# Attention row maxima begun two groups ahead, a first block's last maxima over three PSUM bank pairs, and column sums behind the next projection

## What is computed

```python
xn = group_norm(x, gn_weight, gn_bias)                      # 32 groups
qkv = einsum('oc,bchw->bohw', qkv_weight, xn) + qkv_bias    # 4 heads of 64 channels, 4096 pixels
attn = einsum('bhdk,bhdq->bhkq', q, k) / sqrt(64)
attn = softmax(attn, axis=-1)
out = einsum('bhkq,bhdq->bhdk', attn, v)
out = einsum('oc,bchw->bohw', proj_weight, out) + proj_bias
x1 = x + out        # then BN, relu, 3x3 conv with sign weights, twice, + x1
```

## Time and profile before

| | |
|---|---|
| median of 3 runs | 3069.19 us (3068.3 to 3076.0) |
| profiled execution | 3075.72 us, span 3073.9 us |
| PE busy | 2829.9 us (92%) |
| DVE busy | 2145.2 us (70%) |
| POOL busy | 2025.5 us (66%) |
| ACT busy | 1390.7 us (45%) |
| mean granted TensorE clock | 0.972 |

### The profile page before, as it was taken

The page is one execution under the profiler, slowest core; times in us unless marked ns, Lnnn a source line. Parts: engine busy times, 40 slices in busy tenths (PEclk is TensorE's granted clock), DMA queues, the critical chain, the costliest instruction groups (busy, mean ns, idle before and its releaser), DMA issues. The chain is left out here.

```text
span 3073.9 us, 43595 instructions
## 1 busy us (share of the span) xinstructions
PE 2829.9 (92%) x17060; PEld 1013.5 (33%) x17060; DVE 2145.2 (70%) x2528; ACT 1390.7 (45%) x1461; POOL 2025.5 (66%) x1208
## 2 busy tenths in 40 slices
PE   5799999997999999987999999987999999979898
PEld 3233333323333333333333333342333333334343
DVE  5677777736777777546777777456777776488785
ACT  3354444452545444532544454543454445344342
POOL 2588778783888888843888888855878888520022
PEclk9899999998999999998999999998999999989999
DMA  5000000001000000041000000010000000232032
GB/s 203 33 1 1 1 1 1 1 1 60 1 1 1 1 1 1 1 132 54 1 1 1 1 1 1 1 42 1 1 1 1 1 1 1 71 116 88 0 109 82
DMA packets 26819, 78.27 MB, mean 25 GB/s; under 512 B 1920, under 2 KB 2176, under 8 KB 25600
## 3 DMA queue, kind: packets, MB, share of 16 engines
q1 hardware_dynamic: 25792, 74.19, 6.9%
q10 hardware_dynamic: 832, 1.45, 0.1%
HBM read 58.86 MB, written 16.78 MB: 25 GB/s over the span
## 5 line engine op out<-in xcount | busy, mean ns | idle before, releaser
L492 POOL TENSOR_TENSOR acc_pool<-acc_pool,prob 128x512 f32<-128x512 f32 (+1 forms) x992 | 1779.6, 1794 | 376.9 <-ACT prob L544 269.9
L544 ACT ACTIVATE prob<-ps,exp_scale 128x1024 f32<-128x1024 f32 x1024 | 1091.9, 1111 | 1191.0 <-PE ps L688 1188.5
L788 DVE TENSOR_REDUCE m_part<-ps 128x2 f32<-128x1024 f32 x896 | 1095.2, 1222 | 477.6 <-PE ps L648 453.6
L672 PE MATMUL ps<-prob,vals 128*64 128x512 f32 x4096 | 999.8, 609 | 0.0
L648 PE MATMUL ps<-k_hi,q_hi 64*128 64x512 f16 x1792 | 347.5, 384 | 79.8 <-DVE m_part L788 79.8
L672 PEld LDWEIGHTS ps<-prob,vals 128*64 128x64 f32 x4096 | 250.3, 137 | 498.5 <-issue 367.4
L844 DVE TENSOR_TENSOR ps<-ps,prob 128x512 f32<-128x512 f32 x480 | 331.5, 691 | 91.2 <-ACT prob L544 91.2
L683 PE MATMUL ps<-q_hi,k_hi 64*128 64x512 f16 x2048 | 391.8, 379 | 0.0
L683 PE MATMUL ps<-q_hi,k_lo 64*128 64x512 f16 x2048 | 391.0, 378 | 0.0
L683 PE MATMUL ps<-q_lo,k_hi 64*128 64x512 f16 x2048 | 390.8, 378 | 0.0
L688 PE MATMUL ps<-m_rows,shift 64*128 64x512 f16 x2048 | 390.4, 378 | 0.4
(11 more groups left out here) (115 smaller groups left out, 1587.8 us busy)
## 6 DMA issues: line engine op xcount, KB each, us to landing
xt<-in_x SPq DMA_DIRECT2D x40, 512.0 KB, 4.0
xf<-in_x SPq DMA_DIRECT2D x4, 2048.0 KB, 17.0
x_scratch<-y_tile SPq DMA_DIRECT2D x16, 512.0 KB, 5.0
wf<-in_w_t SPq DMA_DIRECT2D x4, 1152.0 KB, 9.9
rows<-x_scratch SPq DMA_DIRECT2D x8, 576.0 KB, 5.1
rows<-x_scratch SPq DMA_DIRECT2D x8, 544.0 KB, 4.6
xn<-in_x SPq DMA_DIRECT2D x8, 512.0 KB, 5.7
xt<-x_scratch SPq DMA_DIRECT2D x4, 1024.0 KB, 5.1
```

What stands on the lines that cost most here:

```text
L492: nc.gpsimd.tensor_tensor(acc[:, part], acc[:, part], tile[:, part], ALU.add).then_inc(pool_add, 1)
L544: nc.scalar.activation(prob[:, n % PBUF], g.ps_s[:, kt % 2].rearrange("p h n -> p (h n)"), ACT.Exp, scale=g.exp_scale[:]).then_inc(exp_don ...
L672: last = mm(g.ps_o[own[h], :], vals[:, kt, own[h]], prob[:, n % PBUF, h * TB:(h + 1) * TB], start=(kt == 0), stop=(kt == KT - 1))
L788: v.tensor_reduce(m_part[:, :, u], g.ps_max, AX.X, ALU.max).then_inc(mx_used, 1)
```

## The change

- `units_of` gives two units to every group, for the pair's blocks in one sequence that runs LEAD = 2 groups ahead; the third units of groups 6 and 11 are gone, and a block's last unit is reduced in group 13, where `negate_max` now stands. m_part has two slots.
- Projection step kb has the units of key block kb-1, from kb = 1 on; steps 4 to 7 have a fifth ("early") unit, of the next block, between the two matmuls of q. Four units are left behind the last step; they go to ps_max, the two pairs of the score banks, and ps_max again.
- Vectors m_neg go through ps_misc instead of ps_max, so `max_rows` waits for `half_copied`. `copy_half` moves from key tile 1 of the next block to key tile 29 of its own; the 16 halves of DVE are key tiles 11 to 26.
- ACT, not DVE, copies v. ACT normalises a pair's first two inputs ahead of the softmax of block 6 of the pair before. Four small ACT copies per pair are gone.
- A pair's last column sums stand behind the first projection step of the next pair, and at an image's end behind the first two output projections; DVE divides there ahead of the next pair's maxima, and behind the first two residuals.

```diff
-MID_AT = (6, 11)
+LEAD = 2
 ROWS_AT = GROUPS_A - 1
+NEGATE_AT = GROUPS_A - 1 - LEAD
...
+def units_of(qb, group):
+    at = [(qb + 1) * UNITS + 2 * (group + LEAD) + i for i in range(2)]
+    return [(a // UNITS, a % UNITS) for a in at if a < NB * UNITS]
+
+def units_beside(kb):
+    own = [(0, t * NB + kb - 1) for t in range(QT)]
+    return own, [(1, kb - (NB - 2 * LEAD))] if kb >= NB - 2 * LEAD else []
...
-DVE_HALVES = [kt for kt in range(11, KT - 2) if kt not in (15, 20, 25)]
+DVE_HALVES = list(range(11, 27))
+HALF_AT = 29
...
+                act.wait_ge(g.proj_ready, 4 + (pn + 1) * 3)
+                nc.scalar.activation(vals[:, (n2 * 2 + s) * QT:(n2 * 2 + s + 1) * QT, :],
+                                     ps_v[s].rearrange("p (t d) -> p t d", t=QT), ACT.Copy).then_inc(v_copied, 1)
...
                     if kt == 1 and not first:
-                        copy_half(it - 1)
                         copy_output(it - 1)
+                    if kt == HALF_AT:
+                        copy_half(it)
...
                     for qb in range(NB):
+                        if qb == NB - 2 and it0 + NB < 2 * B * NB:
+                            normalize_first((b * 2 + hp + 1) // 2, 1 - hp)
                         softmax(it0 + qb, qb == 0, qb == NB - 1)
...
+                these, early = units_beside(kb) if kb else ([], [])
+                if kb > 1:
+                    pe.wait_ge(hi_ready, 2 * (it0 + kb - 1))
                 for j in range(2):
                     for c in range(CB):
                         ins = mm(g.ps_s[:, s, j], wst[:, c, j, :], xn[:, s, c, :], start=(c == 0), stop=(c == CB - 1))
...
-                        if maxima and c:
-                            first_maxima(it0, n2 - 1, s, [j])
+                        if j == 0 and c == 0:
+                            maxima_of(it0, early)
+                        if kb and c:
+                            if j == 0:
+                                pe.wait_ge(hi_ready, 2 * (it0 + kb))
+                            maxima_of(it0, these[j:j + 1])
...
+            def last_first_maxima(it0):
+                units = units_beside(NB)[0]
+                pe.wait_ge(hi_ready, 2 * (it0 + NB))
+                pe.wait_ge(mx_used, 1 + it0 * UNITS + PLACE[units[0]])
+                maximum(it0, units[0], g.ps_max)
+                maximum(it0, units[1], g.ps_s[:, 0])
+                maximum(it0, units[2], g.ps_s[:, 1])
+                pe.wait_ge(mx_used, 1 + it0 * UNITS + PLACE[units[1]])
+                maximum(it0, units[3], g.ps_max)
...
                     scores(it, qb, kt, first)
-                    next_maxima(it + 1, qb + 1, mid)
                     scores(it, qb, kt + 1, first)
-                    next_maxima(it + 1, qb + 1, early)
+                    maxima_of(it0, units[0:1])
                     if group == ROWS_AT and not last:
+                        pe.wait_ge(half_copied, it + 1)
                         max_rows(it + 1)
...
-                    next_maxima(it + 1, qb + 1, late)
+                    maxima_of(it0, units[1:2])
...
-                    for s in range(2):
-                        project(b, hp, 0, s, False)
+                    project(b, hp, 0, 0)
+                    if hp:
+                        column_sums(it0 - 1)
+                    project(b, hp, 0, 1)
...
-                    for s in range(2):
-                        first_maxima(it0, NB // 2 - 1, s, range(QT))
+                    last_first_maxima(it0)
...
-                    column_sums(it0 + (NB - 1))
...
                     for s in range(2):
                         output_projection(b, n2, s, 1)
+                    if n2 == 0:
+                        column_sums(b * 2 * NB + 2 * NB - 1)
...
+                    if hp:
+                        for part in range(NP):
+                            divide(it0 - 1, part)
+                    for kb in range(1, NB):
+                        project_step(it0, kb)
...
                 for n2 in range(NB // 2):
+                    if n2 == 1:
+                        for part in range(NP):
+                            divide((b + 1) * 2 * NB - 1, part)
                     for s in range(2):
                         residual(b, n2, s)
```

More of the change, by code:

```diff
@@ L595, in _, with project @@
             mm = nc.tensor.matmul
[L597 removed]
+            def project(b, hp, n2, s):
                 it0 = (b * 2 + hp) * NB
@@ L621, in project @@
                                   start=(c == 0), stop=(c == CB - 1))
-                    if maxima and t == 1:
-                        first_maxima(it0, n2 - 1, s, [2])
+                    if t == 1:
+                        maxima_of(it0, these[2:3])
                 last.then_inc(g.proj_ready, 1)
[L625 to L650, removed]
+                maxima_of(it0, these[3:4])
@@ new lines, in maximum, with maxima_of @@
+            def maximum(it0, unit, into):
+                block, u = unit
+                t, kb = u // NB, u % NB
+                for h in range(2):
+                    last = mm(into[:, h], q_hi[own[h], block * TB + t * P:block * TB + (t + 1) * P],
+                              k_hi[own[h], kb * TB:(kb + 1) * TB], start=True, stop=True)
+                last.then_inc(mx_ready, 1)
+            def maxima_of(it0, units):
+                for unit in units:
+                    pe.wait_ge(mx_used, 1 + it0 * UNITS + PLACE[unit])
+                    maximum(it0, unit, g.ps_max)
@@ L848, in query_block @@
                 first, last = qb == 0, qb == NB - 1
+                it0 = it - qb
                 for group in range(GROUPS_A):
-                    mid, early, late = ([], [], []) if last else units_of(group)
-                    next_maxima(it + 1, mid)
-                    next_maxima(it + 1, early)
+                    units = units_of(qb, group)
+                    maxima_of(it0, units[0:1])
                     if group == ROWS_AT and not last:
@@ L858, in query_block @@
                         divide(it - 1, DIVIDE_AT[group, 0])
-                    next_maxima(it + 1, late)
-                    if group == ROWS_AT - 1 and not last:
+                    maxima_of(it0, units[1:2])
+                    if group == NEGATE_AT and not last:
                         negate_max(it + 1)
@@ L864, in query_block @@
                         divide(it - 1, DIVIDE_AT[group, 1])
-                if last:
-                    for part in range(NP):
-                        divide(it, part)
             def residual(b, n2, s):
```

108 lines of the change are left out of this document (48 added, 60 removed).

## The result

The changed kernel takes 2934.47 us (median of 4 runs, 2933.86 to 2936.92), beside 3068.74 us for the kernel before in the same comparison (3060.0 to 3076.0): a ratio of 0.9564, 95% interval 0.9546 to 0.9581. It is faster by 134 us. The forecast was 2932, in a range of 2912 to 2968. The profiled execution of after took 2934.27 us with a span of 2932.5, so the two profiled spans differ by 3073.9 - 2932.5 = 141.4 us, against 139.8 in the sum of the prediction. The mean granted clock rose from 0.972 to 0.988.

A forecast was written before the change was run, and what follows sets the result against it. TensorE (PE), busy 92% of the span, bounds the kernel. Terms -101.3 + 2.7 + 19.2 - 38.8 - 7.6 - 14.0 = -139.8 us take the profiled 3075.7 to 2935.9, lowered to a forecast of 2932 us, range 2912 to 2968.

The forecast's parts named there:

- Steady blocks: Blocks 1 to 6 of each pair: even spacing saves 3.24 us per block, 24 x 3.24 = 77.8 us.
- two times 0.22: Group 15 of a block: PE's cost of the two units that come back there, leaving 3.5 of 3.93 us saved.
- DVE staying late: Second rival: lag behind the division isn't cleared, groups 7 to 13 each pay 0.26 us; time 2987, chance 0.07.
- POOL trailing: Third rival: POOL's fifteen whole tiles in a row slow down and exponentials stall; slower, about 3110 us, chance 0.02.
- The clock dips: Slow-clock spells after group 6's waits in six of 28 blocks end with their cause: 6 x 1.63 = 9.8 us.
- First blocks: First block of each pair, without a division: 2.55 us saved each, four times 10.2 us; cold start left unchanged.
- Early units: Projection steps 4 to 7: an extra unit costs 1.2 us per step, 16 times, +19.2 us.
- The tail: Behind the last projection step: four units instead of eight, 8.0 us for 17.7, saving 9.7, four times 38.8.
- Pair to pair: Last values to next pair's step 2: 16.2 us for 20.0, saving 3.8, twice 7.6 us.
- Done about then or sooner, taken 0: Column sums' wait for POOL's total at a pair end, asked at 5.2 us: 0 to 0.4 us, taken 0.
- Image ends: Output projections begin at the values' end, last residual at 33.0 us behind them; 7.0 us saved, twice 14.0.
- The first rival: Early units and step 1's added wait eat the tail's saving; price 38.5 us, time 2974, chance 0.05.

The follow-up runs named there:

- the two together: The changed kernel with a lead of one group, the negation's factor folded into the mask, and DVE's division one slot earlier: 2920.71 us, ratio 0.9514.

## Why the prediction was right, and where its terms were off

The time was 2.5 us from the forecast, and the cause was the one given: the even spacing carried 91 us, shown by taking it away, the ends 20 and the three bank pairs of the tail some 10. That the shorter tail carries the rest, less what the early units cost, is read from the timeline; only the early units were varied, in the kernels with a lead of one. Point by point:

- **Steady blocks.** 71.12 - 3.24 = 67.88 was worked out, 67.75 measured. The wait that is left is where it was put, at group 6 behind the division: 4.37 from group 5, for 4.13 + 0.26. The 0.1 between the sums is in "two times 0.22": the two groups around the rows grew from 8.48 to 8.80 us, by 0.32 and not by 0.44. The rivals of DVE staying late and of POOL trailing left no trace: there is no wait in groups 7 to 13, and POOL could take 2.2 us more per block without a change of its length.
- **The clock dips** went, all six. Every kernel with even units has none. But the waits alone don't settle it: with them put back there was one dip, not six, so what decides whether a block dips isn't shown.
- **First blocks.** 10.2 us were taken, 13.8 came. Of the 3.6 between them, 1.3 are counting: from the first values to the next rows a first block takes 57.86 us for 60.74, so 2.88 are saved where 2.55 was worked out, because one of the two added units falls behind the rows. The other 2.3 are the cold start, from the rows to the first values: 8.81, 8.83, 10.32 and 8.42 us before, 8.13, 8.37, 8.82 and 8.77 now. "I leave the block's cold start as it is" holds within 0.7 us in three of the pairs (0.68 and 0.46 shorter, 0.35 longer). The 1.5 of the third pair are luck: a start of 10.3 to 10.4 us also turns up once in the kernel with the tail over one pair and once in that of the two together, so it comes and goes. The tail of after is short, and in the first pair its clock is 0.78 in place of the 0.56 of the earlier trace rows, and the first 5 us of the block behind it stand at 0.73 in place of 0.64. The 1 to 2 us per pair that a wholly warm tail was estimated to add were there, 1.0 to 1.7 with the twelve matmuls.
- **Early units.** 1.29 us per step against 1.2, 1.4 us too little over 16 steps.
- **The tail.** 7.46 us against 8.0. The terms were read from a tail with units at 0.61 us; the first ones are at 0.39 now, and the four reductions run back to back in 4.62 us, where 1.22 each would be 4.88. Two units went at once into the score banks, as counted; that this is worth more than 2 us per pair was shown by taking it away.
- **Pair to pair.** This gain was put too high, 17.4 us for 12.3. Step 2 starts 18.15 us behind the values, not 16.2, which is 3.9 us over both ends. "Done about then or sooner, taken 0" was wrong: POOL's total ends 6.2 us behind the values, later than the 5.7 of the earlier trace rows, and PE, which asks at 5.4, idles 0.79. The sums take 655.38 - 654.37 = 1.01 us for 0.95. Step 1 takes 666.31 - 655.38 = 10.93 us for 10.0: the wait of 2.04 for DVE's division was priced, the low clock behind it wasn't (the unit of 663.97 at 0.61 us, the granted clock at 0.50 from 661.96 to 664.04). The last 1.1 us come from the kernel before: of its two pair ends only the first was measured for the forecast, 20.0 us, and the other one takes 18.9.
- **Image ends.** The last residual is at 33.4 and, in the second image, at 34.0 us behind the values, for the forecast's 33.0. The first image end gave 13.4 for 11.9. Up to step 2 it is 6.75 us; another 1.7 come behind it, since in before PE also ran slowly after its wait of 2.91 for x, 2.88 us for four matmuls that take 1.88 elsewhere. The second gave 4.7 for 7.0: of the two image ends before, only the first was measured for the forecast; the second one had 38.7 instead of 40.1.
- **ACT's copies, copy_half, the normalisations** cost nothing that can be seen: ACT's waits for POOL are 7.8 us in all, against 2.2 before, on an engine at 48%. Whether they were needed no run shows; a projection step with four units takes 7.91 us, as before.
- **The first rival**, a projection that gives nothing, had a price of 38.5 us; outside the blocks 34.2 of these came.

These errors have both signs and sum to 1.6 us; the closeness of the total is partly luck, the size of its main term isn't. Lowering the sum's 2935.9 to 2932 wasn't called for either: with the dips gone the changed kernel's times all lie within 3 us of the profiled 2934.27, so the sum's own figure was the nearer one.

## What to carry to other kernels

Before buying a second buffer for a hand-over, compare the round trip (1.7 us here) with the mean interval of the requests (1.95 to 2.18): where the mean is longer, even spacing removes most of the waits, and here it was worth 91 us without one added instruction. Put independent work into a place where an engine waits for another's last total, and price twice what such a hole costs on PE, the idle time and the slower clock behind it. A tiny instruction in the chain between two engines deserves a look at what its neighbour is doing at that moment; the surest cure was to fold it into a constant.

## What the runs showed of the hardware that wasn't expected

A DVE tensor_scalar of 128x8 floats, from SBUF to SBUF, takes 0.17 us alone and up to 1.31 us when it is issued beside a POOL addition of 2.35 us, and it ends within 0.03 us of it, in all 56 cases of two kernels. A tensor_reduce directly ahead of it isn't held up. The Trainium skill (SBUF — State Buffer, Who interferes with whom) says that a tensor_scalar can enter a mode that takes the port pair shared with GpSimd, an exclusive lock that the first to issue holds for its whole instruction, and that a tensor_reduce never does; the three kernels' rows agree with both halves. That the port is the cause is by that rule; the runs show the coincidence of the ends, that moving POOL's tiles brings the delay, and that 31 us come back with the negation gone. The changed kernel pays only 0.03 us, because its negation starts in the last 0.17 us of the addition, and nothing in its source keeps it so.

Twelve matmuls of no use, 2.76 us of PE's time in a hole that was idle anyway, kept the granted clock at 1.00 where it was 0.78 and 0.73, and paid 5.5 us in the four first blocks.
